# A graph network in one launch: the passes over a tile of attention scores stand one slot closer behind the scores

## The reference

```
# layers 0 and 1, per element
h = x @ W
e = leaky_relu(h@a_src [:, None] + h@a_dst [None, :])
p = softmax(where(adj > 0, e, -9e15), axis=-1)
x = layernorm(x + elu(p @ h (+ bias)))
# layer 2, 8 heads
scores = leaky_relu(q @ k.T / 8 + edge_bias[edges])
p = softmax(where(edges > 0, scores, -1e9));  x = layernorm(x + (p @ v over heads) @ Wp + bp)
# layer 3: every pair (i, j) has a sum over 64 features behind a leaky relu
s = u[:, :, None, :] + v[:, None, :, :]
e = einsum('bijf,f->bij', leaky_relu(s), a)
p = softmax(where(adj > 0, e, -9e15));  x = layernorm(x + elu(p @ hp))
```

## Time and profile before

| | |
|---|---|
| median of the runs shown | 8642.15 us (8634.59 to 8649.71, 2 runs) |
| the profiled execution | 8649.23 us, span 8647.4 us |
| busy: TensorE, VectorE, ScalarE, GpSimd | 7735.2, 7484.1, 7400.6, 1498.6 us (89, 87, 86, 17%) |
| TensorE's granted clock, mean | 0.978 |
| idle before the products L783, for DMA | 7.6 us |
| mean of one: vw's copy L1026, q's high half L1017 (ScalarE) | 1.024, 1.104 us |
| mean of one: q's low half L1265 (VectorE) | 1.278 us |

### The profile page before, as it was taken

How to read it: one execution, slowest core, us unless ns; L and a number is a source line. 1 busy time by engine, 2 the same in 40 slices (tenths; PEclk the granted TensorE clock), 3 DMA queues, 4 the chain that set the end, 5 groups by cost and what they waited for, 6 DMA issues and landing times.

```text
span 8647.4 us, 174562 instructions
## 1 busy us (share of the span) xinstructions
PE 7735.2 (89%) x64374; PEld 3572.8 (41%) x64968; DVE 7484.1 (87%) x10867; ACT 7400.6 (86%) x8641; POOL 1498.6 (17%) x582
## 2 busy tenths in 40 slices
PE   4789989899998989989899898998989989898998
PEld 3535344353443534435343343534435344353442
DVE  4789898888889888898888988988889898988888
ACT  2688888888888888888888888888888888988888
POOL 1212121121211112121121211212112121111000
PEclk7999999999999999999999999999999999999999
DMA  3625244262443625335253352534426254362430
GB/s 74 167 57 139 70 110 106 66 144 62 118 94 81 144 55 120 86 87 135 61 125 86 91 123 59 132 75 101 113 60 146 63 118 96 78 145 53 109 77 19
DMA packets 501427, 830.79 MB, mean 96 GB/s; under 512 B 89890, under 2 KB 155426, under 8 KB 500514
## 3 DMA queue, kind: packets, MB, share of 16 engines
q1 hardware_dynamic: 500514, 818.85, 40.9%
HBM read 76.25 MB, written 4.19 MB: 9 GB/s over the span
## 4 chain that ended last, share of the span: by engine, by line
PE 48%; DVE 24%; issue 15%; ACT 7%; DMA 3%; SPq 1%; DVEq 1%; POOL 0%; ACTq 0%; POOLq 0%
PE psum L870 20%; DVE work L1464 12%; PE psum L783 9%; PE psum L745 8%; PE psum L741 4%; DVE work L1302 3%; ACT work L1126 3%; DVE work L1274 3%; ACT work L984 3%; DMA work<-work 2%; ACT work L993 2%; PE psum L707 1%; PE psum L764 1%; SPq L548 1%; PE psum L685 1%
## 5 line engine op out<-in xcount | busy, mean ns | idle before, releaser
L1126 ACT ACTIVATE work<-v,ucol 128x1024 f32<-128x1024 f32 x3727 | 4024.6, 1141 | 392.4 <-PE psum L870 390.8
L870 PE MATMUL psum<-work,pick 128*32 128x512 f32 x32768 | 3923.9, 605 | 239.0 <-DVE work L1464 93.7
L1464 DVE TENSOR_SCALAR work<-v,ucol 128x1024 f32<-128x1024 f32 x4465 | 3397.7, 815 | 225.7 <-PE psum L870 199.4
L870 PEld LDWEIGHTS psum<-work,pick 128*32 128x32 f32 x32768 | 925.4, 110 | 2487.7 <-issue 2058.5
L1274 DVE CUSTOM_DVE_ANT_0 work<-psum,work 128x1024 f32<-128x1024 f32 x1280 | 1544.9, 1207 | 296.1 <-ACT work L984 267.3
L1302 DVE STREAM_TRANSPOSE work<-work 128x1024 f32<-128x1024 f32 x1280 | 1583.5, 1237 | 71.2 <-DMA work<-work 69.7
L984 ACT ACTIVATE work<-psum,beta 128x1024 f32<-128x1024 f32 x1024 | 1139.4, 1113 | 451.9 <-PE psum L745 394.3
L993 ACT ACTIVATE work<-work,least 128x1024 f32<-128x1024 f32 x1280 | 1463.1, 1143 | 3.6 <-DVE least L1274 3.4
L783 PEld LDWEIGHTS psum<-work,vw 128*64 128x64 f32 x16384 | 877.6, 137 | 613.4 <-issue 604.0
L783 PE MATMUL psum<-work,vw 128*64 128x128 f32 x16384 | 1119.2, 279 | 7.6 <-DMA work<-work 7.6
L741 PE MATMUL psum<-mask,ident_b 128*128 128x512 bf16 x1966 | 647.1, 386 | 443.1 <-DVE least L1274 320.0
(11 more groups left out here) (159 smaller groups left out, 5145.3 us busy)
## 6 DMA issues: line engine op xcount, KB each, us to landing
work<-work SPq DMA_DIRECT2D x2560, 256.0 KB, 4.7
adj_in<-in_adj SPq DMA_DIRECT2D x128, 512.0 KB, 5.0
tile3T<-blocks SPq DMA_DIRECT2D x512, 128.0 KB, 2.7
x_in<-in_x SPq DMA_DIRECT2D x16, 256.0 KB, 4.9
xT_both<-in_xT SPq DMA_DIRECT2D x16, 256.0 KB, 5.8
out<-yout SPq DMA_DIRECT2D x16, 256.0 KB, 2.6
work<-in_WqT SPq DMA_DIRECT2D x1, 128.0 KB
work<-in_WkT SPq DMA_DIRECT2D x1, 128.0 KB
```

The costliest lines, as they stand in the source:

```text
L870: mm = pe.matmul(score3[32 * q:32 * q + 32, cols], pick[:, 15 - kk:47 - kk], ring[u % RING][q][:, cols], start=(kk == 0), stop=(kk == 15), ...
L1126: ins = act.activation(ring[u % RING][q], v3[:], ACT.Relu, bias=ucol[:, 4 * T + q, kk:kk + 1])
L1464: ins = dve.tensor_scalar(ring[u % RING][q], v3[:], ucol[:, 4 * T + q, kk:kk + 1], 0.0, ALU.add, ALU.max)
```

## The change

ScalarE's lag behind a tile's slot (`ACT_LAG`) and VectorE's (`DVE_LAG`) go from two slots to one. In slot s ScalarE now does the relu of the tile of slot s-1 and the exps of slot s-2; VectorE the transposition of slot s-3 and the `leaky` of slot s-1; `MOVE_AT` is worked out from `DVE_LAG`, so SyncE's move stands one slot earlier too. The planner counts with the same two constants: its table of units changes for 16 of 127 steps by one unit (slots 8, 9, 16, 17, 46, 47, 52, 82, 83, 104, 106, 112, 114, 122, 124, 143), from 234 to 236 units on ScalarE in all. The slots of scores, products, q, vw, heads and of all other copies stay. A small SBUF tensor is declared that nothing reads or writes.

```
-ACT_LAG, DVE_LAG, Q_LAG = 2, 2, 1
+ACT_LAG, DVE_LAG, Q_LAG = 1, 1, 1
...
         lin3 = sb("lin3", [P, P])
+        top_codes = sb("top_codes", [P, NT])
         top_code = sb("top_code", [P, 2])
```

## The result

| | before | after |
|---|---|---|
| median of the runs | 8642.15 us | 9246.24 us (9243.41 to 9249.08, 2 runs) |
| span of the profiled execution | 8647.4 us | 9241.6 us |
| TensorE's granted clock, mean | 0.978 | 0.956 |

After to before is 1.0702, 95% interval 1.067 to 1.0733: 604 us slower, where 378 were predicted. The time lies above the range's upper end of 9140.

The account below looks back on a forecast made before the run. TensorE was taken to bound slots 84 to 135, VectorE 67 to 83, ScalarE 36 to 43. Terms of 26.3 less 2, so 24.3 us in 15 elements, plus 10 in the first, gave about 9020 us; range 8810 to 9140.

Parts of the forecast that it names:

- the clock: Rival: new TensorE stalls lower its granted clock, 15 us an element or 225 us on top, 9235 us; chance 0.06.
- The edges: Score buffers: unmoved copies and results now stand behind later relus, minimums and ring units, so TensorE waits; terms sum to 26.3 us.
- Slots 108 to 111: Heads: waits for tile 108's minimum +1.6, vw's copy +2.7 and the pair's result +1.4; sum 5.7 us an element.
- 126 to 129: Heads: like those at 108, but two more matmuls in front on TensorE; 5.0 to 5.7, taken as 5.0 us.
- 90 to 93: Heads: minimum sooner, -1.35; transposes cost 2.7 + 1.1, the pair's result +1.4; sum 3.9 us an element.
- q in front of P102: Before TensorE's slot 102 product: q's copies take 10.3 us where TensorE takes 9.06; +1.2 us an element.
- Layer 3's copy: Slots 88 and 118: the copy stands behind a later relu and ring units, TensorE waits; +2.7 and +3.8 us.
- Entry and exit of layer 2's first stretch: Slot 66: units behind tile 67's minimum and vw's copy, +2.5 us; slot 84: one more transposition before q's low half, +1.2.
- Slots 6 to 14 and 36 to 44: ScalarE is full there and its order of work unchanged: 0 us, bounds -3 and +3.
- The 2 us taken back in slots 136 to 159: Element's end: TensorE idles some 4 us for units, which a late TensorE finds ready; 2 us an element subtracted.
- Half: Rival: stalls come, but TensorE regains half from stored units and end idle; 12 us an element, 8830 us; chance 0.12.
- Faster: Rival, faster or equal: buffers emptied sooner, waits for the minimum vanish; 6 us an element, 8555 us; chance 0.08.

Follow-up runs that it names:

- Experiment 5: Changed kernel with matmuls that add zero put in TensorE's waits of slots 88, 109, 111, 118, 127 and 129, half as many as a first try: 9130.28 us.
- Experiment 10: Changed kernel with only ScalarE's lag at one; VectorE's passes and the moves stand where they stood before: 9204.55 us.
- experiment 8: Kernel before the change, with VectorE's layer 3 reduction of slot 92 put behind the tile's passes of that slot: 8614.85 us.
- experiment 1: Changed kernel with all copies that empty the two score buffers, and the pair's result, moved one slot closer too: 8771.55 us.
- experiment 12: Changed kernel with all copies moved closer, and a slot's ring units in front of its tile passes on ScalarE and VectorE: 8680.28 us.

## Why the prediction was wrong

The mechanism was right and its direction too. Two things made it 226 us short: the clock, and smaller terms put at nothing.

**The edges: right.** Experiment 5 shows them in us an element, against before, at the full clock but for the places named. Slots 108 to 111: +5.5 (predicted 5.7). 126 to 129: +4.9 (5.0). 90 to 93: +4.6 (3.9), with 2.9 us more at the lower level than before. q in front of P102: +1.2 (1.2). Layer 3's copy: +3.2 in slots 84 to 87 (2.7) and +4.2 in slots 114 to 117 (3.8). The last two are larger by the same thing, missed: layer 3's product takes a turn in the buffers, so that the next scores need the minimum of the tile directly before them, which now comes late too,

```profile
4151.09 0.60 PE L742 MATMUL psum<-mask,ident_b 128*128 128x512 bf16 x2 [0.56 <-DVE least L1275]
...
4155.84 0.26 ACT L1091 ACTIVATE low<-psum 128x128 f32<-128x128 f32 x1
4156.15 1.03 PE L742 MATMUL psum<-mask,ident_b 128*128 128x512 bf16 x2 [2.51 <-ACT low L1091]
```

(after, slots 87 and 88: 2.51 is the predicted 2.7, the 0.56 in front of it is extra). Entry and exit of layer 2's first stretch, slots 66 to 84, gave +2.9 where 2.5 + 1.2 stood, with another 2.3 in slots 60 to 65 in front of it; these stretches too have 6.3 us more at the lower level than before. The readings that lean on a product shown as x1 (2.82, 9.06, the waits of 1.63 and 2.88) are 0.2 us too long by the missing records, which moves single terms by that much.

**The step that failed: the clock, put at nothing.** The sum takes each new stall at its own length and gives the work behind it no price. The clock was a rival with a chance of 0.06, set aside because "the 2.88 at slot 91 left the clock at 1.00" and "the stalls are split by the transposes". Neither reason held.

The first was read from one element. The same wait of 2.88 us as printed (3.06 in three of them, 2.95 in one) stands at slot 91 in all 15 elements of before. In 11 of them the clock fell in the wait or within 1 us of its end, for 3.4 to 10.2 us; the element of the earlier trace rows is one of the four in which it stayed. Another element and the one of the earlier trace rows, the ten us from the wait's end and the transposes in them:

```profile
2852.07 0.38 PE L741 MATMUL psum<-mask,ident_b 128*128 128x512 bf16 x1 [2.88 <-DVE least L1274]
2853.51 1.91 PE L671 MATMUL psum<-ident,heads_T 128*128 128x128 f32 x8
3916.65 1.04 PE L671 MATMUL psum<-ident,heads_T 128*128 128x128 f32 x8
2852.00:2862.00 10.00, 9.06 (x51) 5.29 (x50) 7.71 (x11) 5.17 (x7) 4.01 (x3) 0.66 0.49 108
3915.00:3925.00 10.00, 7.61 (x56) 4.81 (x58) 9.25 (x14) 6.35 (x9) 3.90 (x3) 1.00 0.49 106
```

Read over all elements, the wait speaks for the rival and not against it.

The second: the wait in front of after's transposes at 4250.61 is 4.36 us with no work in it, with slot 109's scores ahead of it and 1.36 us of wait ahead of those; TensorE was busy 1.26 of 5 us and then got 0.72 of its clock. The split lies behind the longest stall and did not keep the clock up. At the other late copy, after's slots 118 to 120:

```profile
4286.58 0.26 ACT L1091 ACTIVATE yout<-psum 128x128 f32<-128x128 f32 x1
4286.90 1.22 PE L708 MATMUL psum<-xTa,Aq 64*128 64x512 f32 x1 [3.55 <-ACT yout L1091]
4288.90 3.56 PE L871 MATMUL psum<-work,pick 128*32 128x512 f32 x16
```

The half product takes 1.22 (0.69 in the earlier trace rows) and the ring step 3.56 (1.92 in the earlier trace rows): 2.2 us on top of 3.55, the picture of the earlier trace rows that the rival was made from. The rival's price was 15 us an element. Measured: 7.1 an element from experiment 5 (568.3 - 561.2), at 19.2 us less of lower clock (44.4 in after, 25.2 in 5, 15.8 in before, an element), 0.37 for each. For the rest of the added time at the lower clock, 25.2 - 15.8 = 9.4 an element, the same 0.37 makes 3.5, an estimate. Some 10.6 an element, then, 159 us of the 226; the other 67 are 3.8 an element and 10 in the first. Around the waits of 3.55 and 4.36 us the clock fell to 0.50 in all 15 elements of after, for 3.4 or 6.8 us each time. The rival's time, 9235 (by its own terms 9020 + 225 = 9245), came within 11 us of the measured one, partly by luck, since its price was too high by what the next terms were too low.

**Terms put at nothing.** Slots 6 to 14 and 36 to 44 were one term of 0, bounds -3 and +3. They are two: slots 6 to 31 gained 2.1, slots 36 to 43 lost 2.3, and 44 to 52 another 1.2, of which experiment 5 gives 0.5 back. At slot 36 and behind it VectorE (before, then after) and the ring (after) show it:

```profile
3731.60 1.22 DVE L1274 CUSTOM_DVE_ANT_0 work<-psum,work 128x1024 f32<-128x1024 f32 x1 [1.13 <-ACT work L984]
3974.35 1.23 DVE L1275 CUSTOM_DVE_ANT_0 work<-psum,work 128x1024 f32<-128x1024 f32 x1 [3.08 <-ACT work L985]
3985.66 1.93 PE L871 MATMUL psum<-work,pick 128*32 128x512 f32 x16 [1.01 <-DVE work L1465]
```

VectorE now stands 3.08 us in front of layer 1's first minimum, where it stood 1.13, with units queued behind it, and later ring steps wait for these. That is how entry 66 was priced (+2.5); the same step was not taken for slot 36. Experiment 10, with VectorE's lag back at two, has 0.4 left of the 2.3, as one would expect if this is the cause; its table of units differs too. The 2 us taken back in slots 136 to 159 did not come (136 to 141 took 0.6 more, the rest was equal), slots 120 to 123 lost 0.8, and the first element 20 instead of 10 (439.9 to 459.8 us; its time is 436.8 in experiment 8, which leaves it as it is, so 20 is good to a few us).

**The sum.** 24.3 an element were predicted and 38.7 measured. Experiment 5 has 31.6. Its excess of 7.3 is 3.0 at slots 36 to 52, 1.5 at 60 to 83 (5.2 for 3.7), 1.6 at layer 3's two copies and the heads of slot 90, 2.6 for the take-back, 0.8 at slot 120 and 0.4 in slots 0 to 6, less 2.1 at slots 6 to 31, less 0.3 at the other heads and 0.2 in the plain slots.

**The other rivals.** "Half" falls: nothing was given back. "Faster" falls for the whole change, though its two ingredients are real by themselves: layer 0 alone gives 0.5%, the reduction at slot 92 0.3%. With the tile's own passes sooner, layer 0 gained 2.1 us an element (slots 6 to 31); layer 1 lost 2.3 us in slots 36 to 43 though nothing else takes a turn in the buffers between its tiles either; and in layer 2 the time rose, because the copies beside the passes came later: with them moved along too, in experiment 1, 475 of the 604 us came back. Of the signs named in advance, the waits of the transposes for ScalarE came out at 221.4 (100 to 150 named), slots 84 to 135 at 218 (205 named), both on the predicted side and too large, as with the clock. One sign failed: the wait for the minimum was to shrink in slots 67 to 83, and from ring step 66 to 84 it went from 5.8 to 5.3 us an element only. It shrank at slot 91 (4.1 to 1.4 in slots 88 to 99) and in layers 0 and 1 (7.9 to 2.7).

**Open**: the 41 us left in experiment 12; why experiment 10 loses in stretches that before and after both do better, and what its own table of units has in that; why layer 0 gains in slots 6 to 31; how much of the lower clock outside slots 84 to 135 follows from the change.

## To carry to other kernels

When a consumer is moved closer to its producer in buffers that take turns, list every other user of those buffers and move it along, or leave all: 475 of 604 us hung on copies that the diff does not show. Price a new wait on a full TensorE at its length plus what the work behind it pays at the lower clock, look at TensorE's busy time around it and not at the one gap alone (1.26 of 5 us in front of the 0.72 in after), and read the clock behind a wait in every element before calling it harmless; here that work paid some 0.38 us for each us at the lower level. A lag that is one constant for all stretches is worth trying by stretch: one slot closer loses 7% over the whole kernel and gains 0.5% in layer 0 alone.

## What the hardware showed

One and the same wait of 2.88 us (2.7 with the missing record) inside full work, in one and the same program, left the clock at 1.00 in 4 of 15 elements and went with the lower level, 0.50 for 3.4 to 10.2 us, in 11: transposes 1.04 us in one element, 1.91 in another. Behind waits of 3.55 (slot 118) and of 1.36 and then 4.36 us (slot 109) all 15 elements of after had work at the lower level: in the element shown the transposes took 1.38 for 1.09 us and a ring step 3.56 for 1.92. With matmuls that add zero in the waits (experiment 5), none of the 18.4 us an element at the lower level was left in the slots where they stood, and the kernel was faster, 9130 us for 9246, though they did nothing else. Four calls (128x32 weights, 512 columns, float32; x8 in the rows) took some 0.9 us in a row (3.64 us for x32, in a wait of 4.36); at twice the number, 7.07 us for that wait, the whole gain was gone (9251.7 us). And time at the lower clock is not lost one for one: 302 us less of it were worth 116, less than the half that would stand if TensorE were the bound throughout.
